# Causal mask and negated scores written by VectorE's row-maximum pass, in place of a mask matmul

## What is computed

```python
def _attn(q, k, v, causal):
    scale = 1.0 / math.sqrt(q.shape[-1])
    s = jnp.einsum('bhqd,bhkd->bhqk', q, k) * scale
    if causal:
        Tq, Tk = (s.shape[-2], s.shape[-1])
        mask = jnp.tril(jnp.ones((Tq, Tk), dtype=bool))
        s = jnp.where(mask, s, jnp.finfo(s.dtype).min)
    return jnp.einsum('bhqk,bhkd->bhqd', jax.nn.softmax(s, axis=-1), v)
...
a1 = _attn(q, k1, v1, causal=True)
a2 = _attn(q, ks, vs, causal=False)      # 32 selected tokens
a3 = _attn(q, kw, vw, causal=True)
g = gate[:, :, None, None, None]
out = g[:, 0] * a1 + g[:, 1] * a2 + g[:, 2] * a3
```

## Time and profile before

| | us |
|---|---|
| median of 3 runs | 2289.77 |
| lowest and highest | 2286.21, 2292.29 |
| profiled execution, its own time | 2280.42 |
| its span, first to last instruction | 2278.6 |
| mean granted TensorE clock | 0.913 of full speed |

### The profile page before, as it was taken

How to read it: one execution, slowest core, us unless ns; L and a number is a source line. 1 busy time by engine, 2 the same in 40 slices (tenths; PEclk the granted TensorE clock), 3 DMA queues, 4 the chain that set the end, 5 groups by cost and what they waited for, 6 DMA issues and landing times.

```text
span 2278.6 us, 41302 instructions
## 1 busy us (share of the span) xinstructions
PE 1931.2 (85%) x11644; PEld 1110.1 (49%) x11644; DVE 1349.9 (59%) x3206; ACT 1126.1 (49%) x3476; POOL 645.8 (28%) x659
## 2 busy tenths in 40 slices
PE   3333356999989998999899998999899989999995
PEld 2222123555545554555455554555555555555552
DVE  5999942556555555565655564555465645565563
ACT  1112212555546564556555655655465545555551
POOL 0232233333312331333223232323233322332200
PEclk7655665999999999999999999999999999999998
DMA  3000001111101111111111111111111111111101
GB/s 135 0 0 0 0 9 38 51 37 41 48 21 40 39 41 37 34 39 41 44 33 34 46 43 35 34 46 43 35 34 46 43 26 42 36 53 26 41 1 37
DMA packets 71354, 81.39 MB, mean 36 GB/s; under 512 B 29521, under 2 KB 37842, under 8 KB 70994
## 3 DMA queue, kind: packets, MB, share of 16 engines
q1 hardware_dynamic: 71122, 78.55, 13.4%
HBM read 7.70 MB, written 2.10 MB: 4 GB/s over the span
## 4 chain that ended last, share of the span: by engine, by line
PE 74%; DVE 15%; issue 7%; ACT 2%; POOL 1%; SPq 1%; DVEq 1%; DMA 0%; ACTq 0%; POOLq 0%
PE bank L1639 23%; PE bank L1660 14%; PE bank L1601 9%; PE bank L1511 4%; PE bank L1512 4%; DVE arena L1338 3%; PE bank L1641 2%; PE bank L1612 2%; PE bank L1553 2%; PE bank L1507 1%; PE bank L1549 1%; PE bank L1566 1%; DVE arena L1098 1%; DVE arena L1331 1%; PE bank L1574 1%
## 5 line engine op out<-in xcount | busy, mean ns | idle before, releaser
L1331 DVE TENSOR_REDUCE arena<-bank 128x1 f32<-128x512 f32 (+3 forms) x1024 | 501.8, 490 | 681.4 <-PE bank L1641 669.8
L1639 PE MATMUL bank<-arena 96*128 96x512 f32 (+6 forms) x2048 | 782.5, 464 | 44.3 <-issue 33.1
L895 ACT ACTIVATE arena<-bank,arena 128x512 f32<-128x512 f32 (+3 forms) x1024 | 539.7, 527 | 418.3 <-DVE arena L1331 410.9
L1660 PE MATMUL bank<-W,arena 128*128 128x128 f32 x2560 | 480.4, 286 | 38.2 <-DVE arena L1338 33.2
L1660 PEld LDWEIGHTS bank<-W,arena 128*128 128x128 f32 x2560 | 281.3, 142 | 320.9 <-issue 171.3
L1639 PEld LDWEIGHTS bank<-arena 96*128 96x128 f32 x2048 | 336.4, 196 | 189.4 <-issue 146.5
L1338 DVE COPY arena<-bank 128x512 f32<-128x512 f32 (+2 forms) x768 | 351.0, 459 | 0.0
L674 POOL TENSOR_TENSOR arena<-arena,one 128x512 f32<-128x512 f32 x64 | 66.8, 1043 | 846.3 <-DVE arena L1305 836.6
L1641 PE MATMUL bank<-maskB,identB 128*128 128x128 bf16 x1024 | 229.0, 224 | 0.0
L1601 PE MATMUL bank<-arena 128*32 128x256 f32 (+1 forms) x3072 | 222.7, 362 | 3.3 <-DVE arena L1338 2.0
L895 ACT ACTIVATION_READ_ACCUMULATOR arena<-bank,arena 128x1 f32 x1024 | 204.5, 200 | 0.0
(11 more groups left out here) (263 smaller groups left out, 2304.2 us busy)
## 6 DMA issues: line engine op xcount, KB each, us to landing
arena<-arena SPq DMA_DIRECT2D x896, 64.0 KB, 2.0
arena<-arena SPq DMA_DIRECT2D x64, 128.0 KB, 2.4
W<-wide SPq DMA_DIRECT2D x1, 3538.0 KB, 12.9
X<-x SPq DMA_DIRECT2D x8, 256.0 KB, 5.4
out<-arena SPq DMA_DIRECT2D x8, 256.0 KB, 2.2
arena<-arena SPq DMA_DIRECT2D x96, 16.0 KB, 1.9
LW<-lat SPq DMA_DIRECT2D x1, 768.5 KB, 13.9
arena<-mods SPq DMA_DIRECT2D x1, 768.0 KB, 4.4
```

Source lines behind the costliest of these rows:

```text
L895: A(Pb[:, s % 4, 0:n], bank[s % 3][:, lo:lo + n], ACT.Exp, bias=nmax[:, s:s + 1], accum_out=lsum[:, c:c + 1]).then_inc(s_p, 1)
L1331: v.tensor_reduce(nmax[:, s:s + 1], bank[s % 3][:, lo:lo + n], AX_X, ALU.max, negate=True).then_inc(s_max, 1)
L1639: MM(bank[s % 3][:, 0:lo + n], query(t), Kb[a][0:QD, g % 2, h, skip:skip + lo + n], start=True, stop=False)
L1660: last = pe.transpose(bank[3 + k % 2][:, c * P:(c + 1) * P], Pb[:, k % 4, c * P:(c + 1) * P], ident)
```

## The change

VectorE's pass no longer only takes the maximum. It reads the scores from PSUM and a mask from SBUF, adds them, multiplies by -1, writes the result to `Pb[:, s % 4]` and returns the row minimum of what it wrote, which is the negated maximum. The mask matmul and its bf16 constants go. The mask constant becomes 512 columns wide (zero but for the last 128), so that each t takes its last (t + 1) x 128 columns. ScalarE's exponential reads `Pb` and writes it in place, with scale -1. The wait for the transposes of s - 4 moves from ScalarE to VectorE, where a semaphore instruction (`s_seen`) that nobody reads stands ahead of the pass. The scores of s wait for the maximum of s - 3 instead of its probabilities, where s - 3 has no selected keys.

```diff
-        identB = sb("identB", [P, P], BF16)
-        maskB = sb("maskB", [P, P], BF16)
...
+        s_seen = sem("scores_seen")
...
                         act.wait_ge(s_max, u0 + (s + 1))
-                        if not (turn.first and s < 4):
-
-                            act.wait_ge(s_pT, u0 + (s - 3))
...
-                        A(Pb[:, s % 4, 0:n], bank[s % 3][:, lo:lo + n], ACT.Exp, bias=nmax[:, s:s + 1],
+                        A(Pb[:, s % 4, 0:n], Pb[:, s % 4, 0:n], ACT.Exp, bias=nmax[:, s:s + 1], scale=-1.0,
                           accum_out=lsum[:, c:c + 1]).then_inc(s_p, 1)
...
-            step(CP(identB[:], w("ident")))
-            step(CP(maskB[:], w("mask")))
...
                         v.wait_ge(s_qk, u0 + (s + 1))
-                        v.tensor_reduce(nmax[:, s:s + 1], bank[s % 3][:, lo:lo + n], AX_X, ALU.max, negate=True).then_inc(s_max, 1)
+                        if not (turn.first and s < 4):
+
+                            v.wait_ge(s_pT, u0 + (s - 3))
+                        v.sem_inc(s_seen, 1)
+                        v.tensor_tensor_reduce(Pb[:, s % 4, 0:n], bank[s % 3][:, lo:lo + n], w("mask", T - n), -1.0, 3e38,
+                                               ALU.add, ALU.min, nmax[:, s:s + 1]).then_inc(s_max, 1)
...
-                            pe.wait_ge(s_p, u0 + (s - 2))
+                            _, _, a3, t3 = turn.units[s - 3]
+                            pe.wait_ge(s_p if scores_at(a3, t3) else s_max, u0 + (s - 2))
...
                         MM(bank[s % 3][:, 0:lo + n], query(t), Kb[a][0:QD, g % 2, h, skip:skip + lo + n],
-                           start=True, stop=False)
-                        MM(bank[s % 3][:, lo + t * P:lo + n], identB[:], maskB[:], start=False, stop=True).then_inc(s_qk, 1)
+                           start=True, stop=True).then_inc(s_qk, 1)
...
-    mask = np.where(np.arange(P)[None, :] > np.arange(P)[:, None], MASKED, 0.0).astype(np.float32)
+    mask = np.where(np.arange(T)[None, :] - (T - P) > np.arange(P)[:, None], MASKED, 0.0).astype(np.float32)
```

More of the change, by code:

```diff
@@ L35 @@
         ("wfT", P), ("ufT", P), ("wiT", P), ("uiT", P), ("wcT", P), ("ucT", P), ("wo2T", P), ("uoT", P),
-        ("cos", T), ("sin", T), ("mask", P), ("iota", KEEP)]
+        ("cos", T), ("sin", T), ("mask", T), ("iota", KEEP)]
 WIDE_AT, _at = {}, 0
```

## The result

The changed kernel takes 2318.7 us (median of 4 runs, 2316.3 to 2322.6), the kernel before 2288.9 us in the runs beside it: a ratio of 1.0131, 95% interval 1.0111 to 1.0151. It is slower by 30 us where 14 us less were forecast; the time lies inside the range. Each trace is of one execution: before's (2280.4 us) is faster than all its other runs and after's (2322.6 us) is the slowest of its four, so the two traces differ by 42 us where the medians differ by 30.

The account below looks back on a forecast made before the run. TensorE in the attention stage was taken as the bound, its idle time hanging on VectorE's copy. Terms -61.4 + 12.7 + 31.8 + 2.7 = -14.2 us gave 2276 us from the 2289.8 us median, range 2252 to 2322.

Parts of the forecast that it names:

- What bounds the kernel: Attention stage: TensorE sets the pace; its transposes wait for VectorE's copy at 212 of 1024 units.
- The mask: Mask matmul off TensorE's path: 1024 x 0.06 = 61.4 us saved, less 12.7 us where TensorE waits for a copy.
- X: Time added on VectorE between the scores' signal and the copy: 0.15 us, with ends 0.07 and 0.31.
- The accumulator's write-out: Writing out VectorE's accumulated minimum behind the pass: 0.07 us, taken from its smallest passes.
- Who pays it: Transposes waiting for VectorE's late copy: 31.8 us at bound groups plus 2.7 us at near ones.
- bound steps: 212 units whose transposes wait for VectorE's copy, each 0.15 us later: 31.8 us.
- near steps: 38 units whose copy ends about 0.14 us earlier than it must, each losing 0.07 us: 2.7 us.
- A: Rival: fused pass starts late on VectorE, in the bound and near spots; +26 us, 2316 us; chance 0.28.
- B: Rival: no change that can be told, added VectorE time 0.18 to 0.235 us, some 2288 us; chance 0.22.
- D: Rival: VectorE's fused pass runs at half rate; +73 us, 2363 us; chance 0.05.
- C: Rival: 0.09 us ahead of the values' matmuls goes with the mask; 33 us more gain, 2243 us; chance 0.06.
- The exponential's cover: ScalarE's exponential was complete 2.3 us before its transposes at one spot, covering the added delay; without cover, 154 us.

Follow-up runs that it names:

- b_pick22: Kernel before, with VectorE's four picks (128x32 comparisons making one-hot rows of kept keys) issued at step 22 instead of 24: 2287.5 us, ratio 0.9991.
- b_seen_pick22: Kernel before, picks at step 22, wait for the scores moved to a semaphore instruction ahead of VectorE's maximum: 2323.1 us, ratio 1.0147.
- b_nomask_pick22: Kernel before, picks at step 22, mask matmul removed with nothing in its place: 2232.4 us, ratio 0.9737.
- a_mask_pick22: Changed kernel, picks at step 22, mask matmul of before put back behind the scores: 2378.0 us, ratio 1.0385.
- b_copy1: Kernel before, with VectorE's copy of unit s-3 placed ahead of its maximum of s: 2222.6 us, ratio 0.9707.
- a_pick22: Changed kernel, with VectorE's four picks issued at step 22 instead of 24: 2291.9 us, ratio 1.0017.
- a_addlater: Changed kernel, picks left at step 24, GpSimd made to wait for them before its shared-key passes: 2293.1 us, ratio 1.0017.
- a_copy1: Changed kernel, with VectorE's copy of unit s-3 placed ahead of its pass of s: 2204.2 us, ratio 0.9633.
- b_addlater_stall: Kernel before, GpSimd waiting for the picks, and twelve unused comparisons added ahead of them: 2318.8 us, ratio 1.0139.
- b_pick5: Kernel before, with a fifth, unused comparison of the same size ahead of the four picks: 2324.5 us, ratio 1.0169.

## Why the prediction was wrong, step by step

**What bounds the kernel.** Right. TensorE sets the pace, and the transposes' wait for VectorE's copy is where a late pass is paid; moving that copy alone brings 65 us.

**The mask: -48.7 us forecast, -38.1 measured.** The price of 0.06 us was right (0.058), and so was the count of steps that wait for the copy: by the prediction's own measure 220 of 1024 do in b_pick22, and of the 204 of them that stand in the column all but one gain nothing from the mask's removal. But of the other 736 steps there only 618 are 0.058 us shorter; 111 are about as long as before or a little longer. I had taken all that do not wait for the copy as gaining. At some of these places it is a projection that waits for ScalarE, as these rows of the kernel before show, 600 to 2200 us:

```profile
PE bank L1526 <- ACT W L847: 2.4, 6, 0.4
PE bank L1560 <- ACT arena L855: 1.2, 7, 0.2
```

What holds the rest of the 111 is open. The column also leaves out 83 steps; for its 940 the forecast would have been 45 us.

**X: 0.15 us forecast, 0.20 measured.** The separate wait is 0.12 us, not 0.08: the one case of the earlier trace rows was no measure for it. The accumulator's write-out was put at 0.07 us and adds 0.008 us between pass and copy, at all four sizes (607 to 615 ns at 512 columns): its 83 ns lie beside the pass and the copy. The Trainium skill ("VectorE: DVE Perf Modes", section "Two Vector instructions with no wait between them") says that it is an instruction of its own, and the trace agrees (1024 of them); its price by the smallest passes was wrong. The fused pass was put at nothing and is the other 0.07 us: 0.39 us against 0.32 in b_seen_pick22, behind the same kind of wait. (With the mask gone and the maximum left, b_nomask_pick22, the maximum starts 0.629 us after the last score matmul of 512 columns instead of 0.687: just the mask's 0.058, so that part of the prediction held.) All three parts were off, one of them downwards.

**Who pays it.** 34.5 us forecast, 55.6 measured. 0.20 for 0.15 makes the forecast 47. The count of bound steps was right: the 204 of the column pay 40 us in a_mask_pick22, most of them 0.20 us each. What was too small is the term for near steps: 38 at 0.07 us, 2.7 us, where some 130 of the other 736 steps pay a part and a few more than the whole, 16 us in all. A pass that is 0.20 us late uses up the margin of steps that I had put down as free.

**The loop turn: not in the sum, -17.5 us.** Where one turn of the loop goes over into the next, TensorE stands at its next scores with nothing to wait for, before and after:

```profile
PE bank L1639 <- issue: 33.1, 6, 5.9
```

```profile
PE bank L1639 <- issue: 18.4, 7, 4.3
```

All kernels without the mask matmul gain 16 to 20 us there over six passages, all with it gain none (another 3 us, in the step behind it, stand in the column of all others). That it has to do with the 128 instructions fewer in a turn is a guess.

These three terms make -38.1 + 55.6 - 17.5 = 0 us; the changed kernel's own steps and loop turns give 15.0 - 17.9 = -2.9. With all of them right, I would have forecast no change.

**The picks and the clock: not in the sum, +39.3 us.** This is the step that failed: an overlap put at nothing without a reason, and the clock behind it. Of the 39.3 us 7.9 are the longer stall (7 x 1.12), the rest is the clock; by the medians, moving the picks gives back 27. The sum treats the lateness of VectorE as a delay that is paid where TensorE waits for the copy, and every other queue as it was. But the picks stand in the same queue and moved against GpSimd's passes by little more than 0.1 us (GpSimd began 0.34 us behind them, and now 0.21), enough for a second one to be caught. I had read the granted clock as a mean of 0.97 and not looked at which stretches were near falling: before's own dip to 0.77 follows this very place, from 776 us on behind a stall that ends at 771.42.

**Rivals.** A gave 2316 us, the time that came, by another way: X was 0.20, not 0.31, and the bound spots alone would have brought B. That the time lies inside the range is luck: the range reaches so far only by A's X of 0.31. B had the steady part right, D is out by the pass's 690 ns, C since the steps with values' matmuls are 0.058 us shorter and not 0.15. The exponential's cover held.

**What the profile was to show.** Pass near 690 ns: yes. Waits of L1660 for the copy: up from 213 to 433. Start of the pass more than 0.1 us late, then A: 0.19 us, and the sum did turn. Nothing of the list looked at VectorE against GpSimd, or at the clock.

## What to carry to other kernels

When an edit makes an engine a tenth of a microsecond later everywhere, look for the places where its small instructions stand beside GpSimd's passes and where TensorE's clock already dips: 0.15 us of work in seven such places cost as much (37 us by the medians) as a wait that makes every maximum 0.12 us later (36 us). Ask also how much margin a collision still has: here the first was free by 0.07 us and the second was not. Before adding work to a pass, ask what is queued behind it that could go ahead of it; here that order was worth more (65 us) than the edit. And price a wait by whether the instruction carries it itself.

## What was not expected of the hardware

- A wait carried by a semaphore instruction ahead of a VectorE pass: 0.12 us later than carried by the pass; a fused pass with accumulator starts 0.07 us later still.
- A 128x32 comparison of VectorE, 0.23 us alone, takes 1.07 or 1.13 us beside a GpSimd addition on SBUF. A 128x512 pass that reads PSUM and SBUF stood at 0.69 us beside GpSimd's next pass (769.66 against 769.51 us, kernel before).
- How often the granted clock fell to 0.50 behind the picks' place goes with the length of TensorE's stall there, whatever caused it, in the 7 turns of each trace: 0.50 us (b_copy1) and 0.79 us (before, b_pick22) never, 0.90 us (b_seen_pick22) once, 1.10 us (a_pick22, a_addlater) once, 1.28 us (a_mask_pick22) and 1.49 us (a_copy1) three times, 1.53 us (b_addlater_stall) and 1.67 us (b_pick5) four times, 1.97 us (after) six times. What decides between turns with the same stall stays open.
